# Side work of a state-space scan moved to other columns of the ScalarE queue

## The reference

```
B_t, C_t, r_t = x_proj[k] @ u_t                  # 16, 16 and 6 rows
d_t = softplus(dt_proj[k] @ r_t + bias[k])
h_t = h_(t-1) * exp(d_t * A[k]) + d_t * u_t * B_t   # 16 states a channel
y_t = sum over states of h_t * C_t,  + u_t * D[k]
```

## Time and profile before

| | |
|---|---|
| time, median of 3 runs | 16713.96 us (16707.54 to 16715.55) |
| the profiled execution | 16707.54 us, span 16705.6 us |
| VectorE (DVE) busy | 14926.7 us, 89% |
| TensorE (PE) busy | 13571.3 us, 81% |
| GpSimd (POOL) busy | 12620.4 us, 76% |
| ScalarE (ACT) busy | 12298.3 us, 74% |
| mean granted TensorE clock | 0.933 |

### The profile page before, as it was taken

How to read it: one execution, slowest core, us unless ns; L and a number is a source line. 1 busy time by engine, 2 the same in 40 slices (tenths; PEclk the granted TensorE clock), 3 DMA queues, 4 the chain that set the end, 5 groups by cost and what they waited for, 6 DMA issues and landing times. The chain is left out here.

```text
span 16705.6 us, 189354 instructions
## 1 busy us (share of the span) xinstructions
PE 13571.3 (81%) x38048; PEld 5620.9 (34%) x38048; DVE 14926.7 (89%) x20527; ACT 12298.3 (74%) x27189; POOL 12620.4 (76%) x6313
## 2 busy tenths in 40 slices
PE   7988978888888878888888886877777777777777
PEld 2222223333333333333333333533333333333333
DVE  6666669999999988999999996889999988999998
ACT  3555567777777766777777774588888968888996
POOL 0000059999999978999999994289999968999996
PEclk9999989999999999999999998988888888888988
DMA  1100023333333333333333332122222212222221
GB/s 24 19 14 17 5 74 113 112 113 112 111 111 111 111 96 107 112 113 113 111 111 111 111 111 80 49 78 85 85 84 83 84 48 80 85 85 84 83 84 46
DMA packets 543207, 1404.94 MB, mean 84 GB/s; under 512 B 135566, under 2 KB 191926, under 8 KB 539430
## 3 DMA queue, kind: packets, MB, share of 16 engines
q1 hardware_dynamic: 542034, 1392.84, 29.0%
HBM read 1311.24 MB, written 58.30 MB: 82 GB/s over the span
## 5 line engine op out<-in xcount | busy, mean ns | idle before, releaser
L1415 POOL TENSOR_TENSOR Tr<-du,BC 128x1344 f32<-128x1344 f32 x2688 | 8174.7, 3041 | 138.5 <-DVE du L1283 137.2
L1079 PE MATMUL PS<-Hc,ident 128*128 128x448 f32 x16128 | 7115.6, 578 | 1363.7 <-POOL Hc L1424 1133.9
L1079 PEld LDWEIGHTS PS<-Hc,ident 128*128 128x128 f32 x16128 | 3063.8, 199 | 5308.9 <-issue 2706.6
L1200 ACT ACTIVATE PS<-dl,A 128x448 f32<-128x448 f32 x5376 | 3401.9, 633 | 1599.8 <-DVE Hr L1333 1054.9
L1424 POOL TENSOR_TENSOR Hc<-Hr,BC 128x448 f32<-128x448 f32 (+1 forms) x2688 | 3603.9, 1341 | 602.2 <-DVE Hr L1333 527.1
L1333 DVE TENSOR_TENSOR_SCAN PS<-PS,Tr 128x449 f32<-128x449 f32 x3584 | 3711.0, 1078 | 93.0 <-ACT st L1216 82.4
L1340 DVE TENSOR_TENSOR Hc<-PS,BC 128x448 f32<-128x448 f32 x4480 | 2568.9, 607 | 0.0
L1210 ACT ACTIVATE PS<-cs,lneps,A 128x448 f32<-128x448 f32 x2688 | 1935.1, 720 | 18.8 <-DVE PS L1333 1.0
L1333 DVE TENSOR_TENSOR_SCAN Hr<-PS,Tr 128x449 f32<-128x449 f32 x1792 | 1938.4, 1082 | 0.0
L1333 DVE TENSOR_TENSOR_SCAN Hr<-Ar,PS 128x449 f32<-128x449 f32 x1792 | 1931.7, 1078 | 0.0
L1315 DVE SCALAR_TENSOR_TENSOR PS<-PS,Tr 128x448 f32<-128x448 f32 x2688 | 1651.1, 614 | 223.2 <-ACT PS L1210 203.6
(11 more groups left out here) (271 smaller groups left out, 15394.8 us busy)
## 6 DMA issues: line engine op xcount, KB each, us to landing
BC<-bcscratch SPq DMA_DIRECT2D x5376, 224.0 KB, 3.6
zscratch<-zst SPq DMA_DIRECT2D x84, 224.0 KB, 1.9
bcscratch<-rows SPq DMA_DIRECT2D x336, 56.0 KB, 1.7
z<-zscratch SPq DMA_DIRECT2D x28, 672.0 KB, 4.8
xg<-mid SPq DMA_DIRECT2D x12, 1176.0 KB, 7.9
xr<-mid SPq DMA_DIRECT2D x56, 168.0 KB, 2.7
rl<-rows SPq DMA_DIRECT2D x56, 168.0 KB, 3.3
Q<-part SPq DMA_DIRECT2D x72, 98.0 KB, 4.4
```

Source lines behind the costliest of these rows:

```text
L1079: e.matmul(PS[:, YB + c, 0:T], K["ident"][:], Hc[:, g % NHC, c, :], start=False, stop=(nn == 15)).then_inc(y_done, 1)
L1200: e.activation(decay_at(u, 1), dl[:, q % 2, c, :], ACT.Exp, scale=A[:, q // NT, c, nn:nn + 1]).then_inc(a_done, 1)
L1415: e.tensor_tensor(Tr[:, g % NTR] if ratio else Tr[:, g % NTR, :, 1:TW], du[:, q % 2], b, ALU.mult).then_inc(t_done, 1)
```

## The change

The tables go; the columns are written as ranges, mostly the same for both kinds. No operation is added or taken away.

| | L1 before | L1 after | L3 before | L3 after |
|---|---|---|---|---|
| merge | 0, 1, 3 | 0, 1, 2 | 1, 2, 4 | 0, 1, 2 |
| gather | 4, 6, 7 | 3, 4, 5 | 5, 7, 8 | 3, 4, 5 |
| keep_dts, keep_rows | 10, 11 | 7, 8 | 10, 11 | 7, 8 |
| absolute | 13, 16, 19 | 10, 13, 16 | 13, 17, 21 | 10, 13, 16 |
| positive | 14, 17, 20 | 11, 14, 17 | 14, 18, 22 | 11, 14, 17 |
| expo | 15, 18, 21 | 12, 15, 18 | 16, 20, 23 | 12, 15, 18 |
| one_plus | 22, 23, 25 | 19, 20, 21 | | |
| minus_w | 24, 27, 30 | 22, 23, 24 | | |
| loga | 26, 28, 31 | 25, 26, 27 | 25 (all) | 24 (all) |
| delta | 29, 35, 41 | 31, 35, 40 | 32, 36, 41 | 31, 35, 40 |
| VectorE's one_less | | | 26 | 22 |
| VectorE's inputs / cumsum | 31, 37, 42 | 32, 36, 41 | 33, 37, 42 | 32, 36, 41 |
| TensorE's proj (round) | 3 | 2 | 3 | 2 |
| pre_delta | 4, 5, 6 | 3, 4, 5 | 4, 5, 6 late | 3, 4, 5 |
| total | 9, 10 late, 12 late | 9 late, 11, 12 late | 10, 11, 12 late | 9 late, 11, 12 late |

The first tile, which has no scans beside it, is prepared by the same function, in L1 in the order of a list `FIRST` (all of c = 0, then of c = 1, then of c = 2) instead of stage by stage.

```
+FIRST = [3, 4, 5, 7, 8] + [s for c in range(3) for s in (10 + 3 * c, 11 + 3 * c, 12 + 3 * c, 19 + c, 22 + c, 25 + c)] + [31, 35, 40]
...
 # TensorE
-                if r == 3:
+                if r == 2:
                     proj(q)
-                elif r in (4, 5):
-                    pre_delta(q, r - 4)
...
+                elif 3 <= r < 6:
+                    pre_delta(q, r - 3)
+                elif r == 11:
+                    total(q, 1)
+
+            def prepare_late(q, r):
+                if r == 9:
                     total(q, 0)
...
 # ScalarE
+                if 3 <= s < 6:
+                    gather(q, s - 3)
+                elif s == 7:
+                    keep_dts(q)
+                elif s == 8:
+                    keep_rows(q)
+                elif s in (10, 13, 16):
+                    absolute(q, s // 3 - 3)
...
-                if q and s in MERGE:
-                    merge(q - 1, MERGE.index(s))
+                if q and s < 3:
+                    merge(q - 1, s)
                 if q + 1 < NQS:
                     prepare(q + 1, s)
+                    if ratio and s == 24:
+                        for i in range(3):
+                            loga(q + 1, i)
...
 # VectorE
-                if ratio and s == 26:
+                if ratio and s == 22:
                     one_less(q)
-                elif s in AFTER:
-                    (cumsum if ratio else inputs)(q, AFTER.index(s))
+                elif s in (32, 36, 41):
+                    (cumsum if ratio else inputs)(q, (32, 36, 41).index(s))
```

More of the change, by code:

```diff
@@ L1049, in prepare @@
             def prepare(q, r):
-                if r == 3:
+                if r == 2:
                     proj(q)
-                elif r in (4, 5):
-                    pre_delta(q, r - 4)
[L1054 to L1058, removed]
+                elif 3 <= r < 6:
+                    pre_delta(q, r - 3)
+                elif r == 11:
                     total(q, 1)
             def prepare_late(q, r):
[L1062 to L1065, removed]
+                if r == 9:
+                    total(q, 0)
                 elif r == 12:
@@ L1164, in prepare @@
             def prepare(q, s):
[L1166 to L1184, removed]
+                if 3 <= s < 6:
[6 more added lines that the diff above has]
+                    absolute(q, s // 3 - 3)
+                elif s in (11, 14, 17):
+                    positive(q, s // 3 - 3)
+                elif s in (12, 15, 18):
+                    expo(q, s // 3 - 4)
+                elif not ratio and 19 <= s < 22:
+                    one_plus(q, s - 19)
+                elif not ratio and 22 <= s < 25:
+                    minus_w(q, s - 22)
+                elif not ratio and 25 <= s < 28:
+                    loga(q, s - 25)
+                elif s in (31, 35, 40):
+                    delta(q, (31, 35, 40).index(s))
             def merge(q, c):
@@ L1236, in act @@
                 e.preload_act_table_set("natural_log_exp_and_others")
[L1237 to L1249, removed]
+            for s in range(48) if ratio else FIRST:
+                if s == 10:
+                    e.wait_ge(c_ld, 48)
+                prepare(0, s)
+                if ratio and s == 24:
+                    for c in range(3):
+                        loga(0, c)
             if not ratio:
@@ L1302, in prepare @@
             def prepare(q, s):
-                if ratio and s == 26:
+                if ratio and s == 22:
                     one_less(q)
-                elif s in AFTER:
-                    (cumsum if ratio else inputs)(q, AFTER.index(s))
-            AFTER = (33, 37, 42) if ratio else (31, 37, 42)
+                elif s in (32, 36, 41):
+                    (cumsum if ratio else inputs)(q, (32, 36, 41).index(s))
             def input2(u):
```

## The result

The changed kernel takes 16967.68 us (median of 4 runs, 16965.33 to 16982.6), the kernel before 16714.75 us (4 runs): 1.0152 times as long, 95% interval 1.0137 to 1.0168, or +253 us. The forecast was 16905 us and slower, its range 16800 to 17005. The sign, the range and the parts on L1 hold. The sum is 60 us too low: a term that it leaves out is worth 97 us, and a clock term with the wrong sign in L3 hides some 40 of them. The profiled execution took 16968.33 us; that of the kernel before, 16707.54, is the fastest of its 4 runs.

The account below looks back on a forecast made before the run. It took VectorE's scans as the bound, stopped only by waits for ScalarE. Terms 78 (L1) + 92 (L3) + 15 + 18 (clock) - 10 (prologue) = +193 us gave 16907, stated as 16905; 80% range 16800 to 17005.

Parts of the forecast that it names:

- Step 1: In L1, keep_dts two columns behind the last gather waits: +0.62 us per diagonal, +0.73 transposed, +0.87 contiguous tile, 78 us.
- Step 2: L3: nine operations in a row cost 0.70 us, logarithms in column 0 3.2, less 2.83 before: +1.07 per tile; L1 nothing.
- Step 3: L3's first groups: moved merges and gathers cost transposed tiles +0.9 us; merges close behind TensorE add 0.15 contiguous, 0.25 transposed.
- Step 4: Longer TensorE idleness makes more projections run at 1.2 GHz: +15 us in L3, +18 us in L1's contiguous tiles.
- Step 5: L1's first tile, finished column by column, runs two of three totals under ScalarE's work: about -5 us a pair, -10.
- Absorbed: Rival: the scans' stops vanish in slack or early projection results, so no real change: +21 us, 16735; chance 0.05.
- The clock everywhere: Rival: nearly every tile's projection runs at 1.2 GHz and keep_dts stands 1.67 us longer: +317 us, 17030; chance 0.12.
- Faster: Rival: the 0.32 us wait for the last delta goes, 48 us, with the prologue 58: 16656; chance 0.03.

## Why the prediction came out as it did

**What bounds the kernel** (right). What VectorE loses in the scans is in the end time: the stages' differences sum to 254 us beside 260.7 of span.

**Step 1, the distance from gather to `keep_dts` in L1** (right). +0.65 and +0.72 us per diagonal and transposed tile where +0.62 and +0.73 were written, and by the same mechanism; the runs with L1 alone (+99) and with L1's copies alone (-20) isolate it. In contiguous tiles with a fast projection, groups 0 to 3 lose 0.98 us where 0.87 was written.

**Step 2, the dense run and the logarithms** (right in its terms). Groups 5 and 6 lose 0.62 us together, forecast 0.70; group 8 loses 3.26, forecast 3.2. One `du` product a tile waits 0.32 us, the third before and the second after, as written, and L1's denser run costs nothing: its groups 3 to 9 last 4.02 to 4.05 us.

**What failed** is in the sentence of step 2 that compares the middle parts: "So 0.70+3.2-2.83 = +1.07 per tile". The sum has no term for `one_less`, which moves from s=26 to s=22, and so treats it as taking the same time of VectorE at both places. That time was 0.97 us in the kernel before, where groups 7 and 8 are 3.80 us over 2·5.07 and 2.83 of it were read as stops. There VectorE would have stood waiting for the weight anyway. At s=22 nothing covers it (ScalarE waits with it), and it starts behind GpSimd's product and takes 1.93 us more: group 7 is 7.77 us instead of 5.07, 2.70 where 0.97 was implied. Groups 7 and 8 together went from 3.80 us over to 5.96, +2.16 where 3.2-2.83 = +0.37 was in the sum. That is 1.79 us per tile, 97 us over the 54 tiles. Moved one column on, 134 us came back. The prediction asks of ScalarE's operations what covers them, and never of this one of VectorE.

**Step 3, L3's merges and gathers** (nearly right). It gave +0.15 us to contiguous and +1.15 to transposed tiles, walked in tiles with a fast projection. Among such tiles groups 0 to 3 went from 0.0 to 0.26 us over 4·5.06 in contiguous and from 1.42 to 2.24 in transposed ones, +0.25 and +0.82: 29 us where 35 was written.

**Step 4, the clock** (right in L1, wrong in sign in L3). In L1 the direction and about the size: 14 of 24 contiguous projections slow where 4 in 10 were taken, so +1.73 us a tile against 1.54, and the idle time of TensorE ahead of them rose from 1.05 to 2.28 us in the median, as forecast. In L3 the sentence "The new distance lengthens TensorE's idleness ahead of the projection: L3 transposed from 2.6 to about 4 us" fails. The idle time fell, from 2.98 to 2.04 us in the median of the transposed tiles and from 1.96 to 1.41 in the contiguous ones. The slow projections fell with it, from 17 of 28 to 12 and from 10 of 24 to none, where 2 in 3 were taken. A fast one of a contiguous and a slow one of a transposed tile, with the granted clock over each at 1.00 and 0.58:

```profile
11374.94 2.48 PE L1032 MATMUL PS<-xs,xp 128*76 128x448 f32 x6 [1.40 <-ACT xs L1110]
...
12752.61 4.17 PE L1032 MATMUL PS<-xs,xp 128*76 128x448 f32 x6 [2.04 <-ACT xs L1110]
```

A slow one costs its tile 1.3 to 1.6 us, about as priced (1.4). So this term was a gain of some 24 us where +15 was written, and that miss of 39 us hid part of the 97 of `one_less`. Without it the time would have been near 17007, at the upper end of the range: that it lies well inside is luck in part. The idle time ahead of the projection isn't all that decides: in the kernel before, the ten slow contiguous projections of L3 stand behind 1.91 to 1.99 us of it and the fourteen fast ones behind 1.90 to 1.99, and the earlier trace rows already had 2.57 us before a fast one and 1.91 before a slow one. What else decides is open.

**Step 5, the prologue** (a little high). 2.3 us in the first call and 5.1 in the second, for 5 each. The third `du` product waits 2.38 us for the last `delta` as in the earlier trace rows, and only the second of the three totals came under ScalarE's work (first call):

```profile
2322.82 0.62 DVE L1277 TENSOR_TENSOR du<-PS,xs 128x448 f32<-128x448 f32 x1 [0.65 <-ACT dl L1158]
2325.83 0.62 DVE L1277 TENSOR_TENSOR du<-PS,xs 128x448 f32<-128x448 f32 x1 [2.38 <-ACT dl L1158]
```

**The rivals.** Absorbed: no, VectorE waits 129.6 us for `keep_psum` in L1. The clock everywhere, 17030 us: no, slow projections are none of 56 in diagonal and 3 of 28 in transposed L1 tiles (1 before). That price has half of the other L1 tiles slow; with all of them, as the rival is worded, it would be about 17100. The Trainium skill's rule of a throttled start in every tile ("TensorE: Matmul & The Clock Gate", section HAM oscillation) holds in 14 of the 24 contiguous L1 tiles and hardly elsewhere in L1. Faster: no, the 0.32 us stop stays, it only moves from group 14 to group 12.

## What to carry to other kernels

An operation that is free where it stands is free because something covers it; when it moves, find the cover first, and look at what the engine that shares its memory ports does at the new place. In a queue served in order, the distance between the last input of a matmul and the operation that reads its result must hold the matmul at its slow clock, and not only at its fast one. When a wait is taken away at one side operation, look at the next in the chain before the gain is booked.

## What the runs showed of the hardware

One VectorE tensor-scalar of 128x1344 f32 in SBUF took 833 ns where no GpSimd instruction was running as it began, 2764 ns when a GpSimd product of 3.02 us had begun 0.98 us ahead of it, and 1282 ns when one of 1.93 us had 0.58 us left. Begun 0.17 us ahead of a GpSimd product of 1.93 us, it lengthened that to 2.45; begun 0.54 us ahead of one that takes 3.04 us elsewhere, to 3.65. VectorE's scans, which run beside the same GpSimd products all the time, took 1.08 us at either place and weren't touched.

Six matmuls of the projection took 2.48 us at a granted clock of 1.00, or some 4.1 us at 0.58 to 0.60, behind idle times of TensorE that overlap: 2.29 us ahead of a 4.10, 2.57 us ahead of a 2.48, and both kinds behind 1.9 to 2.0 us in L3 before. Two matmuls behind 2.51 us took 1.86 instead of 1.01 at 0.50, and the lower clock lasted through the six that followed them, 4.83 us instead of 2.52 at 0.51.

A table load of ScalarE took 1.28 us with no idle time ahead of it, and three logarithms of 448 columns between two loads kept the queue for 4.4 us.
